# A residual added by an accumulating transfer, and one product split between VectorE and GpSimd, in a two-layer attention, mixture-of-experts and state-space kernel

## The reference

```python
xn = _layernorm(x, axis=-1)
h = xn @ fc1_w.T + fc1_b
xc, z = jnp.split(h @ in_proj_w.T, 2, axis=-1)
u = silu(conv4(xc) + conv_b)                      # 4 taps along the sequence
dt_low, Bm, Cm = jnp.split(u @ x_proj_w.T, [16, 32], axis=-1)
dt = softplus(dt_low @ dt_proj_w.T + dt_proj_b)
# over the sequence, 512 channels x 16 states:
hstate = exp(dt_t * A) * hstate + (dt_t * u_t) * B_t
y_t = sum over states of hstate * C_t
s = (((y + u * D) * silu(z)) @ out_proj_w.T) @ fc2_w.T + fc2_b
g = silu((silu(xn @ wg.T) * (xn @ wu.T)) @ wd.T)
x = x + s * g
```

## Time and profile before

| | |
|---|---|
| Median of 3 runs | 2803.9 us (2802.91 to 2807.53) |
| The profiled execution | 2805.47 us |
| Its span, first to last instruction | 2803.7 us |
| Second layer's scan, first slot to the last product with C | 909 us to 2779 us |
| Length of one period in it (q = 2 to 15) | 117.1 us |
| Busy over the span | PE 2542.8, DVE 2322.1, POOL 2060.7, ACT 2013.0 us |

### The profile page before, as it was taken

The page is one execution under the profiler, slowest core; times in us unless marked ns, Lnnn a source line. Parts: engine busy times, 40 slices in busy tenths (PEclk is TensorE's granted clock), DMA queues, the critical chain, the costliest instruction groups (busy, mean ns, idle before and its releaser), DMA issues.

```text
span 2803.7 us, 37402 instructions
## 1 busy us (share of the span) xinstructions
PE 2542.8 (91%) x13454; PEld 1489.0 (53%) x13454; DVE 2322.1 (83%) x2883; ACT 2013.0 (72%) x3253; POOL 2060.7 (74%) x682
## 2 busy tenths in 40 slices
PE   7897899999976899999999999999999999999978
PEld 3454344443443565656656566565655646556455
DVE  7685777777634999898998989989899898998995
ACT  4222466666634788787888978889788897888864
POOL 0656011111211999999999999999999999999996
PEclk9898899999978899999999999999999999999989
DMA  6347988888641131321313213132131321313210
GB/s 187 116 117 188 247 226 229 201 202 219 218 154 72 79 129 47 113 106 38 129 47 113 106 38 129 47 113 106 38 129 47 113 105 40 129 42 110 98 46 8
DMA packets 129505, 323.86 MB, mean 116 GB/s; under 512 B 15757, under 2 KB 84365, under 8 KB 112798
## 3 DMA queue, kind: packets, MB, share of 16 engines
q1 hardware_dynamic: 107050, 249.05, 28.9%
q0 software_dynamic: 19968, 71.38, 8.0%
q10 hardware_dynamic: 2304, 1.05, 0.2%
HBM read 286.75 MB, written 43.13 MB: 118 GB/s over the span
## 4 chain that ended last, share of the span: by engine, by line
POOL 32%; PE 20%; issue 13%; DVE 3%; ACT 1%; DMA 0%; POOLq 0%; DVEq 0%; SPq 0%; ACTq 0%
POOL l_st L1710 15%; POOL l_st L1702 9%; PE l_p_w L2163 6%; PE l_p_w L2104 5%; PE l_p_y L2088 5%; POOL keep_xg L1710 4%; POOL l_dtu L1716 2%; PE l_p_w L2182 2%; DVE l_st L1515 1%; POOL l_gate L1726 1%; DVE keep_xg L1515 1%; DVE keep_xg L1524 1%; PE l_p_w L2170 1%; PE l_p_w L2111 0%; ACT l_p_a L1798 0%
## 5 line engine op out<-in xcount | busy, mean ns | idle before, releaser
L1515 DVE TENSOR_TENSOR_SCAN l_st<-l_p_a,l_hl,l_st 128x512 f32<-128x512 f32 x768 | 932.3, 1265 | 105.7 <-ACT l_p_a L1798 95.5
L1710 POOL TENSOR_TENSOR l_st<-l_st,lw_cs 128x2048 f32<-128x2048 f32 x192 | 869.1, 4544 | 0.0
L1798 ACT ACTIVATE l_p_a<-l_dt,lw_a_neg 128x512 f32<-128x512 f32 x1024 | 664.9, 680 | 45.6 <-DVE keep_xg L1515 37.9
L1702 POOL TENSOR_TENSOR l_st<-l_bs,l_dtu 128x2048 f32<-128x2048 f32 x128 | 581.4, 4542 | 28.8 <-PE l_p_y L2088 25.4
L2088 PEld LDWEIGHTS l_p_y<-keep_ident,l_st 128*128 128x128 f32 x3072 | 354.4, 145 | 145.7 <-POOL l_st L1710 79.3
L2088 PE MATMUL l_p_y<-keep_ident,l_st 128*128 128x128 f32 x3072 | 384.4, 281 | 48.6 <-POOL l_st L1710 48.3
L1020 ACT ACTIVATE a_pr<-a_p_s 128x512 f32<-128x512 f32 x512 | 284.8, 596 | 145.8 <-PE a_p_s L1089 142.0
L931 DVE TENSOR_REDUCE a_mpart<-a_p_m 128x1 f32<-128x512 f32 x512 | 312.2, 681 | 14.1 <-PE a_p_m L1045 13.0
L1515 DVE TENSOR_TENSOR_SCAN keep_xg<-l_p_a,l_hl,keep_xg 128x512 f32<-128x512 f32 x256 | 314.7, 1266 | 1.6
L1710 POOL TENSOR_TENSOR keep_xg<-keep_xg,lw_cs 128x2048 f32<-128x2048 f32 x64 | 291.1, 4549 | 2.0 <-ACT l_hl L1803 2.0
L858 POOL DMA_DIRECT2D a_w<-in_w_dram x32 | 23.1, 725 | 328.8 <-PE a_p_m L1119 273.4
(11 more groups left out here) (246 smaller groups left out, 4027.3 us busy)
## 6 DMA issues: line engine op xcount, KB each, us to landing
l_bs<-s_bc SPq DMA_DIRECT2D x64, 1024.0 KB, 4.7
lw_cs<-s_bc SPq DMA_DIRECT2D x64, 1024.0 KB, 4.7
a_w<-in_w_dram POOLq DMA_DIRECT2D x32, 1024.0 KB, 11.7
late<-in_w_dram POOLq DMA_DIRECT2D x32, 1024.0 KB, 18.9
kx<-s_kp SPq DMA_DIRECT2D x96, 256.0 KB, 11.3
keep_share<-s_x SPq DMA_DIRECT2D x32, 512.0 KB, 5.1
s_kp<-late SPq DMA_DIRECT2D x96, 128.0 KB, 2.1
s_vp<-late SPq DMA_DIRECT2D x16, 544.0 KB, 3.5
```

What stands on the lines that cost most here:

```text
L1515: eng.tensor_tensor_scan(st[k % NG][:, n, :], p_a[:, n, :], st[k % NG][:, n, :], hl[:, k, n:n + 1], ALU.mult, ALU.add).then_inc(scan_ok, 1)
L1702: eng.tensor_tensor(st[n][:, :, :], bs[:, 4 * n:4 * n + 4, :], dtu[(k // NG) % 2][:, :].unsqueeze(1).broadcast_to([P, NG, TT]), ALU.mult). ...
L1710: eng.tensor_tensor(st[n][:, :, :], st[n][:, :, :], cs[:, 4 * n:4 * n + 4, :], ALU.mult).then_inc(cm_ok, 1)
L1798: eng.activation(p_a[:, n, :], dt[c % 2][:, :], ACT.Exp, scale=a_neg[:, c, m:m + 1]).then_inc(dA_ok, 1)
```

## The change

Two edits. First, the scratch tensor for the first layer's result is gone: the first layer writes its rows into the output tensor itself, SP reads tiles from there, and GpSimd issues a transfer that adds `gate` to the rows of the output in HBM (`accum_op=ALU.add`). SP's load of the old rows and its store go, except for the last tile, which keeps VectorE's two halves. SP's load of tile q+1's rows now waits only for PE's transposes of tile q.

Second, the product of slot 9 is split. VectorE makes its first two states, GpSimd the other two. VectorE's `scan_unit` waits for VectorE's half before state 0 and for GpSimd's before state 2.

```diff
-                    eng.dma_start(scr["x1"][part, :].rearrange("(p a) d -> p (a d)", p=P),
+                    eng.dma_start(scr["out"][part, :].rearrange("(p a) d -> p (a d)", p=P),
...
-                    eng.indirect_dma_start(scr["x1"], bass.IndirectOffsetOnAxis(target[:, k:k + 1], 0), xo[:, k, :], None,
+                    eng.indirect_dma_start(scr["out"], bass.IndirectOffsetOnAxis(target[:, k:k + 1], 0), xo[:, k, :], None,
...
+        DRIVE_V, HALVED = (0, 2, 4, 6, 8, 9, 10, 12, 14), (9,)
+        def drives(t, k):
+            return t * len(DRIVE_V) + sum(1 for x in DRIVE_V if x <= k)
+        def driven(eng, t, k, n):
+            if k % 2 == 0 or (k in HALVED and n < 2):
+                eng.wait_ge(dbu_v, drives(t, k))
+            else:
+                eng.wait_ge(dbu_g, t * 8 + k // 2 + 1)
...
                     if end:
-                        if front:
-                            filled(eng, "tr", q, 1)
-                        eng.dma_start(xt[:, :, :], rows(scr["x1"], f)).then_inc(old_in, 16)
-                        if f < NT - 1:
-                            eng.wait_ge(res_ok, f + 1)
-                            eng.dma_start(rows(scr["out"], f), gate[:, :, :]).then_inc(out_st, 16)
-                        else:
+                        if f == NT - 1:
+                            eng.dma_start(xt[:, :, :], rows(scr["out"], f)).then_inc(last_io, 16)
...
                     if nxt:
                         if front:
                             filled(eng, "tr", q, 1)
-                        eng.dma_start(xt[:, :, :], rows(scr["x1"], q + 1)).then_inc(x_in, 16)
+                        eng.dma_start(xt[:, :, :], rows(scr["out"], q + 1)).then_inc(x_in, 16)
...
                 def scan_unit(s, k, n):
                     g = s * SLOTS + k
                     eng.wait_ge(dA_ok, g * NG + n + 1)
+                    if n == 0 or (k in HALVED and n == 2):
+                        driven(eng, s, k, n)
                     if n == 0:
-                        eng.wait_ge((dbu_v, dbu_g)[k % 2], s * 8 + k // 2 + 1)
...
-                    eng.tensor_tensor(st[n][:, :, :], bs[:, 4 * n:4 * n + 4, :],
-                                      p_u[:, :].unsqueeze(1).broadcast_to([P, NG, TT]), ALU.mult).then_inc(dbu_v, 1)
+                    many = 2 if k in HALVED else NG
+                    eng.tensor_tensor(st[n][:, 0:many, :], bs[:, 4 * n:4 * n + many, :],
+                                      p_u[:, :].unsqueeze(1).broadcast_to([P, many, TT]), ALU.mult).then_inc(dbu_v, 1)
...
                         step_size(s, 3)
+                        dbu(s, 9)
                         scan_unit(s, 9, 0)
...
-                    eng.tensor_tensor(st[n][:, :, :], bs[:, 4 * n:4 * n + 4, :],
-                                      dtu[(k // NG) % 2][:, :].unsqueeze(1).broadcast_to([P, NG, TT]), ALU.mult).then_inc(dbu_g, 1)
+                    first = 2 if k in HALVED else 0
+                    eng.tensor_tensor(st[n][:, first:NG, :], bs[:, 4 * n + first:4 * n + 4, :],
+                                      dtu[(k // NG) % 2][:, :].unsqueeze(1).broadcast_to([P, NG - first, TT]), ALU.mult).then_inc(dbu_g, 1)
...
                 def residual(t):
                     taken(eng, "op", t, 1)
-                    eng.wait_ge(old_in, t * 16 + 16)
-                    eng.tensor_tensor(gate[:, :, :], gate[:, :, :], xt[:, :, :], ALU.add).then_inc(res_ok, 1)
+                    eng.dma_start(rows(scr["out"], t), gate[:, :, :], accum_op=ALU.add).then_inc(out_st, 16)
```

More of the change, by code:

```diff
@@ L1376, in layer1_stage @@
         bs = sb("bs", [P, NST, TT])
-        x_in, old_in, out_st, bc_st = sem("x_in"), sem("old_in"), sem("out_st"), sem("bc_st")
+        x_in, last_io, out_st, bc_st = sem("x_in"), sem("last_io"), sem("out_st"), sem("bc_st")
         b_in_ok = [sem(f"b_in{n}") for n in range(NG)]
@@ L1436, in period @@
                     if end:
-                        if front:
-                            filled(eng, "tr", q, 1)
-                        eng.dma_start(xt[:, :, :], rows(scr["x1"], f)).then_inc(old_in, 16)
-                        if f < NT - 1:
-                            eng.wait_ge(res_ok, f + 1)
-                            eng.dma_start(rows(scr["out"], f), gate[:, :, :]).then_inc(out_st, 16)
-                        else:
+                        if f == NT - 1:
+                            eng.dma_start(xt[:, :, :], rows(scr["out"], f)).then_inc(last_io, 16)
                             for h in two:
-                                eng.wait_ge(res_ok, f + h + 1)
-                                eng.dma_start(rows(scr["out"], f)[:, 2 * h:2 * h + 2, :], gate[:, 2 * h:2 * h + 2, :]).then_inc(out_st, 16)
+                                eng.wait_ge(res_ok, h + 1)
+                                eng.dma_start(rows(scr["out"], f)[:, 2 * h:2 * h + 2, :], gate[:, 2 * h:2 * h + 2, :]).then_inc(last_io, 16)
                     if nxt:
@@ L1457, in load_b @@
                             if scan:
-                                eng.wait_ge((dbu_v, dbu_g)[n % 2], s * 8 + (12 + n) // 2 + 1)
+                                driven(eng, s, 12 + n, 2)
                             eng.dma_start(bs[:, 4 * n:4 * n + 4, :].rearrange("p n t -> p (n t)"),
@@ L1481, in _ @@
                 tiles(eng, period)
-                eng.wait_ge(out_st, 16 * (NT + 1))
+                eng.wait_ge(out_st, 16 * (NT - 1))
+                eng.wait_ge(last_io, 16 * 3)
             @block.vector
@@ L1566, in last_residual @@
                 def last_residual(h):
-                    eng.wait_ge(old_in, NT * 16)
+                    eng.wait_ge(last_io, 16)
                     taken(eng, "op", NT - 1, h)
@@ L1861, in step_input @@
                     eng.wait_ge(dtu_ok, t * CB + c + 1)
-                    wait(eng, dbu_v, t * 8 + 2 * c)
+                    wait(eng, dbu_v, drives(t, 4 * c - 1))
                     eng.activation(p_u[:, :], dtu[c % 2][:, :], ACT.Copy).then_inc(dtp_ok, 1)
@@ L2295, in build_program @@
         "oe": scratch("oe", (B, NE, D)),
-        "x1": scratch("x1", (B * S, D)),
         "bc": [scratch(f"bc{p}", (2 * NST, TT)) for p in range(2)],
```

## The result

The changed kernel takes 2787.84 us (median of 4 runs, 2787.14 to 2788.93), the kernel before, measured beside it, 2804.34 us (4 runs, 2802.91 to 2807.53). The ratio is 0.9944, 95% interval 0.9932 to 0.9956: 16.5 us less, where 22 were forecast. The direction and the range held, and so did the time of the forecast's own case (2775 to 2788, by 0.2 us); its gain of 1.0 to 1.9 us a period did not.

The account below looks back on a forecast made before the run. The prediction took GpSimd, in a loop with PE, as the bound: 14 x 1.42 = 19.9 us plus 1.0 and 1.1 made 22.0, for 2782 us. The range ran from 2758 to 2799 us.

Parts of the forecast that it names:

- the forecast's own case: PE's sums of slot 9 decide GpSimd's gain: 1.0 to 1.9 us a period, 2775 to 2788 us; chance 0.44.
- What bounds the kernel before: GpSimd bounds the 117.06 us period, a second engine close behind; loop of GpSimd's 82.6 us and PE's 34.4.
- The residual, 1.64 gained: On GpSimd, the addition's 2.34 us gives way to a transfer issue of 0.70 us, gaining 1.64 (1.0 to 1.8).
- The halves: Slot 9's product: GpSimd takes 2.34 us instead of 4.49, saving 2.15; VectorE is given 1.15 us with start-up.
- The first limit: GpSimd's slot 9 product waits for PE's sums of slot 5: 0.75 of 1.64 us passes, 2.9 gained behind it.
- some 0.6: Sign in the profile after: a GpSimd gap of that many us ahead of slot 13's product, ended by PE.
- The second limit: GpSimd's slot 13 product waits for PE's sums of slot 9: 1.02 us, plus PE 0.40 earlier, 1.42 gained.
- That is just enough: Behind slot 13's weighed, VectorE about 0.35 us later against PE fits 0.25 of room and 0.18 of own wait.
- VectorE takes it back: Rival: VectorE arrives 1.4 us later than worked out, PE's part grows, within 5.6 us of 2804; chance 0.17.
- a loop without GpSimd: Rival: VectorE's 1.15 us lies in a ScalarE and PE loop with too little slack, 2810 to 2817 us; chance 0.05.
- held until the transfer landed: Rival: GpSimd stands 9.0 us until the accumulating transfer lands, losing 4.5 us a period, 2871 us; chance 0.08.
- The ends: Outside the fourteen loops: 1.0 us credited to the first period and 1.1 to the last; last tile's end unchanged.

Follow-up runs that it names:

- the run without the issue: Changed kernel with dummy products in PE's idle time; SP stores gate plainly, GpSimd issues no transfer, residual left out: 2785.39 us, ratio 0.9926.
- The kernels with one state: Changed kernel with dummy products on PE, slot 9 split one state VectorE, three GpSimd: 2781.10 us; with next tile's statistics also moved earlier on VectorE: 2777.33 us.

## Why the prediction was right and wrong, point by point

**What bounds the kernel before: right.** GpSimd's loop of 117.1 us. The second engine "close behind" was VectorE: its own loop, with the residual's addition gone from GpSimd, is 114.90 without the added product, 2.19 under GpSimd's.

**The residual, 1.64 gained: 1.1 in truth, without effect.** The next instruction starts 0.79 us behind the issue (forecast 0.70), but the four that follow are 0.5 longer together, and the whole is 1.27 by the run without the issue. It was within the bounds (0.51 to 1.3). Since only 0.75 was held to pass the wait at slot 9, the term of the sum stayed right: 0.76. The wait there was 0.24 for this reason (1.07 - 0.76 = 0.31 with the true size); the prediction's own numbers made 1.64 - 0.75 = 0.9 of it, not the 0.6 that it named.

**The halves: right.** 2.35 on GpSimd (2.34 to 2.38). On VectorE 1.30 from start to start instead of 1.15.

**The first limit: right.** Behind slot 9 GpSimd gains 0.75 + 2.15 = 2.9. By the prediction's sum 2.9 - 1.42 = 1.5 of that had to turn up as a wait ahead of slot 13, and 1.43 did; the "some 0.6" that it gave as the sign is a slip against its own sum. The kernels with one state bear the slope out (1.06 for 1.08 us).

**The second limit: right in kind, off in size.** The step that was off is VectorE's lateness. Slot 9's first scan stands 0.75 late against the frame of before (forecast 0.70), ScalarE's copy of block 1's sum 0.77, but the sums of slot 8 are 0.25 earlier, not 0.40, and those of slot 9 0.14. PE also has a wait there that the prediction lacked, 0.81 for ScalarE to empty the bank of a gate block (row 1905.30). GpSimd got 1.15 at slot 13 where 1.42 was forecast.

**"That is just enough": wrong.** The prediction put VectorE 0.35 us late behind `weighed` of slot 13, with 0.43 of room. It is 0.69 late. Against slot 5's product, VectorE is 0.75 late at slot 9 and makes it good by slot 13, where it starts when it did before. From there it has one wait, ahead of slot 15, and that gives only 1.60 - 1.16 = 0.44, while GpSimd and PE are 1.15 earlier. PE waits 0.23 and its stretch takes about 0.3 longer. With the 0.27 missing at slot 13 that is the difference between 1.42 and 0.87 along this path. The cause is VectorE alone, by the runs: 1.27 us taken from GpSimd ahead of slot 9 left the period as it was, so did 0.20 more of waiting ahead of slot 13 where the clock fell, and 1.30 taken from VectorE came out of it in full. By the prediction's own sign, a new gap of PE behind the sums of slot 13, its mechanism was wrong here.

**The rivals.** "VectorE takes it back" (0.17) came true in part: it took 0.55 of 1.42. What happened is the mechanism of the last one, "a loop without GpSimd", at another size: I put its slack at 1.4 and gave it 0.05 as a cause of a loss. The slack was 117.09 - 114.90 = 2.19. Less the 1.30 added, 0.89 is left, and 0.87 is what the change gained. That sum is the short form of the whole case. It holds with both edits together; the split alone gained 0.32. Nothing was held until the transfer landed: it lands 6.0 us after issue and GpSimd goes on after 0.79.

**The ends.** First period 1.0 forecast and nothing found; last period and end 1.1 forecast, 3.3 - 0.7 = 2.6 found; 1.5 ahead of the second layer is not of the change. That the total came nearer to the forecast (16.5 of 22) than the period (0.87 of 1.42) is luck: without the ends' surplus and the 1.5 it would be some 14.

## What to carry to other kernels

When work goes from the bound engine to its neighbour, work out the neighbour's own loop first: its slack against the period, less the work added, is the most that can be gained, whatever the first engine saves. A wait is not slack if what it waits for moves with the addition: the half at slot 9 cost its 1.30, and at slot 13, with a wait of 1.14 us behind it, still 1.08. Ahead of slot 6 the wait does take in most of what is put there: 1.38 us of statistics moved into it took 0.95 off the period. And look at PE's granted clock in each experiment: where less work elsewhere leaves the period unchanged to 0.1 us, a fall of the clock may stand in the place of what was taken away. And a kernel that another engine holds, as the one with slot 7 halved, does not show what an addition costs.

## What the hardware showed that I had not expected

**An accumulating transfer on GpSimd.** 512 runs of 1 KB: its instruction and its landing in the changed kernel:

```profile
L1736 POOL DMA_DIRECT2D out_dram<-l_gate x15: 1236/1282/1437, 1060.6 to 2684.5; - x15
...
DMA to landing us min/median/max: 5.6/6.0/6.3
```

The next instruction starts after 0.79 us, but those up to the next wait show 0.5 us more than their usual length (5.05, 5.07 and 9.55 instead of 4.57, 4.56 and 9.07 in the kernel without it), so GpSimd loses 1.27 in all. A plain store of this size landed in 3.2 us, this one in 6.0. The Trainium skill, page "DMA: Bandwidth & Descriptors", section "Anatomy of one DMA — SWDGE (gpsimd) path", has a fit of 2.0 us and the bytes at 436 GB/s, which gives an estimate of 3.2 us here; for the accumulating form the measured 6.0 decides.

**PE's clock within a dense period.** PE was busy for 95% of a period, and still its granted clock fell to 0.50 for 3.4 us in eight of the changed kernel's periods, behind an idle time of 1.06 us, and did not fall in the others, which look the same in all rows before. What the difference between such periods is stays open. The falls in the changed kernel begin 116.05 us apart (1547.4, 1663.4, 1779.5) and its periods are 116.22 long, so each stands 0.17 us earlier in its period than the one before; that this ends them was not tried. The price of a fall was nothing in the changed kernel, the kernel before and the one with the transfer alone, 0.47 us in the kernel with one state on VectorE (116.15 less 115.68) and 1.27 in the one with none (116.18 less 114.91).
